# Weight copies moved to ScalarE, more idle products in the front, and three result tiles added by TensorE in a one-core language-model tower

## The reference

```python
h = emb(x) + b + positions
h = h + gelu(2 * Re(xs @ C~) + D * u)        # u = layernorm(h), xs = scan of Lambda_bar over time
x = layernorm(h)
logits = x @ router_w.T + router_b           # top 2 of 8 experts, softmax of the two
h1, h2 = split(x @ fc1_w[e].T + fc1_b[e])    # 256 each
y = (silu(h1) * h2) @ fc2_w[e].T + fc2_b[e]
h = h + sum over the token's 2 experts of weight * y
```

## Time and profile before

| | us |
|---|---|
| median of 3 runs | 154.09 |
| the three runs | 153.95, 154.09, 155.47 |
| the profiled execution's own time | 154.8 |
| its span (first to last instruction) | 153.1 |
| PE / DVE / ACT / POOL busy | 121.7 / 114.4 / 73.3 / 91.7 |
| mean granted TensorE clock (1 is full) | 0.899 |

### The profile page before, as it was taken

One profiled execution on the slowest core, in us unless ns is written; L12 is line 12 of the kernel. 1 busy time (PEld: TensorE's weight loads), 2 busy tenths in 40 slices (PEclk: granted clock), 3 DMA queues, 4 the chain that ended last, 5 costly groups with the idle time before them and its releaser, 6 DMA issues.

```text
span 153.1 us, 3532 instructions
## 1 busy us (share of the span) xinstructions
PE 121.7 (80%) x807; PEld 96.7 (63%) x807; DVE 114.4 (75%) x481; ACT 73.3 (48%) x236; POOL 91.7 (60%) x113
## 2 busy tenths in 40 slices
PE   0088889988699949966877999999999999999200
PEld 0033357476479617843765799999999999972000
DVE  2988899998994899697476768677777787735573
ACT  2063462463273142256263466878778778760000
POOL 5777779101774477157757777777777777674000
PEclk9999999986975895699999999999999999997555
DMA  4422121991441261135224414433433011100997
GB/s 106 131 52 50 38 51 34 220 297 40 148 150 52 52 227 47 44 88 116 60 75 118 91 52 113 119 106 107 121 79 82 24 42 47 54 33 0 288 310 224
DMA packets 15093, 15.65 MB, mean 102 GB/s; under 512 B 2995, under 2 KB 11701, under 8 KB 15074
## 3 DMA queue, kind: packets, MB, share of 16 engines
q1 hardware_dynamic: 10914, 9.39, 23.4%
q0 software_dynamic: 2784, 5.28, 10.8%
q10 hardware_dynamic: 1376, 0.77, 1.7%
HBM read 9.62 MB, written 6.27 MB: 104 GB/s over the span
## 4 chain that ended last, share of the span: by engine, by line
PE 23%; issue 9%; DVE 6%; POOL 6%; DMA 5%; DVEq 1%; SPq 1%; ACT 1%; POOLq 0%; ACTq 0%
PE bank L1220 7%; PE bank L1206 7%; PE bank L1196 6%; POOL results L363 6%; DMA yres<-results 3%; DVE act_h L752 1%; PE bank L1186 1%; DMA results<-ysb,dest 1%; SPq L279 1%; DVEq L738 1%; DVE res L844 1%; DVE res L848 1%; PE bank L1076 1%; ACT rows L904 1%; DVE arg L634 0%
## 5 line engine op out<-in xcount | busy, mean ns | idle before, releaser
L352 POOL DMA_INDIRECT sorted_rows<-rows,slot x32 | 32.3, 1010 | 27.2 <-DVE slot L654 18.2
L741 DVE COPY w1b<-w_sb 128x516 f32 x39 | 18.5, 476 | 13.2 <-issue 5.3
L752 DVE SCALAR_TENSOR_TENSOR act_h<-bank,w1b,sil 128x128 f32<-128x128 f32 x78 | 23.6, 343 | 5.0 <-PE bank L1206 1.4
L363 POOL DMA_INDIRECT results<-ysb,dest x22 | 21.7, 986 | 7.9 <-issue 7.3
L1220 PE MATMUL bank<-w_sb,act_h 128*128 x156 | 24.7, 281 | 1.5 <-issue 1.0
L1206 PE MATMUL bank<-xT,w1b 128*128 128x128 f32 x156 | 24.1, 277 | 1.5 <-DVE act_h L752 1.4
L953 ACT ACTIVATE sil<-bank,w1b 128x128 f32<-128x128 f32 x78 | 24.4, 364 | 0.1
L1196 PE MATMUL bank<-xT,w1b 128*128 128x128 f32 x156 | 24.0, 276 | 0.0
L1220 PEld LDWEIGHTS bank<-w_sb,act_h 128*128 128x128 f32 x156 | 20.5, 191 | 2.7 <-issue 2.6
L1206 PEld LDWEIGHTS bank<-xT,w1b 128*128 128x128 f32 x156 | 20.5, 192 | 2.1 <-DVE act_h L752 2.1
L944 ACT COPY xT<-bank 128x128 f32<-128x128 f32 x39 | 10.3, 265 | 22.4 <-PE bank L1186 22.3
(11 more groups left out here) (231 smaller groups left out, 185.5 us busy)
## 6 DMA issues: line engine op xcount, KB each, us to landing
w_sb<-w_all SPq DMA_DIRECT2D x8, 386.0 KB, 4.9
xt<-sorted_rows SPq DMA_DIRECT2D x39, 65.0 KB, 1.9
yres<-results SPq DMA_DIRECT2D x8, 256.0 KB, 4.7
sorted_rows<-pad SPq DMA_DIRECT2D x1, 520.0 KB, 5.9
sorted_rows<-rows,slot POOLq DMA_INDIRECT x32, 2.8
out<-res SPq DMA_DIRECT2D x2, 256.0 KB, 3.9
results<-ysb,dest POOLq DMA_INDIRECT x22
results<-ysb,xt POOLq DMA_INDIRECT x17
```

The costliest lines, as they stand in the source:

```text
L352: gp.indirect_dma_start(sorted_rows[:, :], bass.IndirectOffsetOnAxis(ap=slot[:, k, t:t + 1], axis=0), rows[:, k, t, :], None).then_inc(s_s ...
L363: gp.indirect_dma_start(results[:, :], bass.IndirectOffsetOnAxis(ap=target, axis=0), ysb[i][:, :], None, bounds_check=bound, oob_is_err=Fa ...
L741: v.tensor_copy(w1b[i % 4][:, :], w_sb[:, bass.ds(at, W1)]).then_inc(s_wb, 1)
L752: v.scalar_tensor_tensor(act_h[i % 2][:, q], ps_l[sides(i)][:, q], w1b[i % 4][:, 2 * HID + 2 + c:2 * HID + 3 + c], sil[i % 2][:, q], ALU.a ...
```

## The change

Three things at once.

1. The nine weight copies of the first list (tiles 0 to 8) are made by ScalarE, not VectorE. ScalarE waits for the table of tile numbers and for the weights, loads nine register values in one go, copies tile 0's weights before `gelu(3)`, those of 1 and 2 after it, of 3 after `turn_copy(2)` and before `normed_x(3)`, and of tile i+3 in the loop for i = 1 to 5, before `keep(i - 1)`. VectorE starts with tile 9.
2. `idle_products` are put in: 3 after `turn_u(2)`, 6 after `skipped(2)`, 3 after `logits(1)`, 11 where 3 stood before `turn_x(2)` (a wait that stood there is gone), 5 after `list_tiles(0)`, 4 where 1 stood before `rotated(3, 0)`.
3. Tiles 36 to 38 are no longer scattered and loaded back (`SPREAD` is 3, `STORED` 36). GpSimd makes counting rows, VectorE makes a 0/1 matrix for each of the 3 tiles and 4 groups (`spread_tile`, 128x512 each), and TensorE adds `spread.T @ ysb` into the PSUM bank of the group's bias term, 4 products of 128x128x128 fp32 for each tile and group. As rows that only these tiles hold are no longer written, SP first fills `results` (2 MB) with zeros from a tile that VectorE clears; GpSimd waits for that before its first result. The bias terms use four banks; VectorE's additions now go group by group.

```diff
+SPREAD = 3
+STORED = NTILES - SPREAD
-        ps_add = [banks[0], banks[6]]
+        ps_add = [banks[0], banks[6], banks[2], banks[5]]
...
+            sp.wait_ge(s_zero, 1)
+            sp.wait_ge(s_gath[1], 16 * GT)
+            sp.dma_start(results[:, :].rearrange("(p q j) d -> p q (j d)", p=P, j=GT),
+                         zeros[:, None, :].to_broadcast([P, K * NT // GT, GT * D])).then_inc(s_empty, 16)
             sp.wait_ge(s_const, 3)
...
-            sp.wait_ge(s_ys, 16 * NTILES)
+            sp.wait_ge(s_ys, 16 * STORED)
...
+            gp.iota(iota_j[:, :, :], [[1, GT], [GT, P]], base=0, channel_multiplier=0,
+                    allow_small_or_imprecise_dtypes=True).then_inc(s_iotaj, 1)
...
+            pool.wait_ge(s_empty, 16)
             scatter_result(0)
             scatter_result(1)
             scatter_rows(NG - 1)
-            for i in range(2, NTILES):
+            for i in range(2, STORED):
                 scatter_result(i)
...
+            def last_tokens():
+                dve.wait_ge(s_dest, chunk_of(NTILES - 1) - chunk_of(EARLY) + 1)
+                dve.wait_ge(s_iotaj, 2)
+                step(v.tensor_copy(last_d[:, :], dest[:, LATE - SPREAD:LATE]))
+                step(v.tensor_scalar(last_h[:, :], last_d[:, :], TOKENS - 0.5, -float(TOKENS), ALU.is_gt, ALU.mult))
+                step(v.tensor_tensor(last_d[:, :], last_d[:, :], last_h[:, :], ALU.add))
+                v.tensor_tensor(last_g[:, :, :], last_d[:, :, None].to_broadcast([P, SPREAD, NG]),
+                                iota_g[:, None, :].to_broadcast([P, SPREAD, NG]), ALU.subtract).then_inc(s_last, 1)
+
+            def spread_tile(n, g):
+                dve.wait_ge(s_last, 1)
+                v.tensor_scalar(spread[:, n, g, :], iota_j[:, :, :].rearrange("p j t -> p (j t)"),
+                                last_g[:, n, g:g + 1], None, ALU.is_equal).then_inc(s_spread, 1)
...
-            dve.wait_ge(s_table, 2)
-            dve.wait_ge(s_w, 16 * NE)
-            expert_weights(0)
-            expert_weights(1)
...
-                if i + 2 < NTILES:
+                if FULL[0] <= i + 2 < NTILES:
...
+                if i == CHUNKS[-2]:
+                    last_tokens()
+                if i == NTILES - 2:
+                    for t in range(SPREAD):
+                        spread_tile(t, 0)
+
+            for g in range(1, NG):
+                for t in range(SPREAD):
+                    spread_tile(t, g)
             for g in range(NG):
                 add_bias(g)
-            for g in range(NG):
                 dve.wait_ge(s_added, g + 1)
...
+            def first_list():
+                act.wait_ge(s_table, 2)
+                act.wait_ge(s_w, 16 * NE)
+                return nc.values_load_multi_w_load_instructions(
+                    tile_wi[0:1, 0:FULL[0]], engines=[mybir.EngineType.Activation], min_val=0, max_val=(NE - 1) * WE,
+                    skip_runtime_bounds_check_because="starts of an expert's weights, made from the expert's number")[1]
+
+            def copy_weights(i):
+                if i >= 4:
+                    act.wait_ge(s_a, 2 * i - 6)
+                a.copy(w1b[i % 4][:, :], w_sb[:, bass.ds(starts[i], W1)]).then_inc(s_wa, 1)
...
+            starts = first_list()
+            copy_weights(0)
             gelu(3)
+            copy_weights(1)
+            copy_weights(2)
...
                 if i == 0:
+                    copy_weights(3)
                     normed_x(3)
                     copy_xnT(3)
+                if 1 <= i and i + 3 < FULL[0]:
+                    copy_weights(i + 3)
...
             turn_u(2)
+            idle_products(3, ps_xT[1])
             b_times_u(2)
             skipped(2)
+            idle_products(6, ps_xT[1])
             turn_x(1)
             logits(1)
+            idle_products(3, ps_xT[1])
             rotated(2, 0)
...
-            pe.wait_ge(s_xnT, 4)
-            idle_products(3, ps_xT[1])
+            idle_products(11, ps_xT[1])
             turn_x(2)
             logits(2)
             list_tiles(0)
+            idle_products(5, ps_xT[1])
             pe.wait_ge(s_rotin, NG)
-            idle_products(1, ps_vs)
+            idle_products(4, ps_vs)
...
+            def spread_result(n, g):
+                pe.wait_ge(s_oe, STORED + n + 1)
+                pe.wait_ge(s_spread, SPREAD * g + n + 1)
+                for j in range(GT):
+                    ins = te.matmul(ps_add[g][:, j * D:(j + 1) * D], spread[:, n, g, j * P:(j + 1) * P],
+                                    ysb[STORED + n][:, :], start=False, stop=(n == SPREAD - 1 and j == GT - 1))
+                if n == SPREAD - 1:
+                    ins.then_inc(s_corr, 1)
...
+                if i == NTILES - 2:
+                    mixed_bias(0)
             for g in range(NG):
-                mixed_bias(g)
+                if g >= 1:
+                    mixed_bias(g)
+                for t in range(SPREAD):
+                    spread_result(t, g)
```

More of the change, by code:

```diff
@@ L190, in lm_tower @@
         ysb = [sb(f"ysb{i}", [P, D]) for i in range(NTILES)]
+        zeros = sb("zeros", [P, GT * D])
+        iota_j = sb("iota_j", [P, GT, P])
+        iota_g = sb("iota_g", [P, NG])
+        last_d = sb("last_d", [P, SPREAD])
+        last_h = sb("last_h", [P, SPREAD])
+        last_g = sb("last_g", [P, SPREAD, NG])
+        spread = sb("spread", [P, SPREAD, NG, GW])
         yres = sb("yres", [P, K, NT, D])
@@ L217, in lm_tower @@
         s_corr = sem("s_corr"); s_added = sem("s_added")
+        s_zero = sem("s_zero"); s_empty = sem("s_empty"); s_iotaj = sem("s_iotaj"); s_last = sem("s_last"); s_spread = sem("s_spread")
         s_norm = sem("s_norm"); s_un = sem("s_un"); s_uTp = sem("s_uTp"); s_uT = sem("s_uT")
@@ L226, in lm_tower @@
         s_xt = [sem(f"s_xt{i}") for i in range(NTILES)]
-        s_tp = sem("s_tp"); s_te = sem("s_te"); s_wb = sem("s_wb"); s_gate = sem("s_gate"); s_lin = sem("s_lin")
+        s_tp = sem("s_tp"); s_te = sem("s_te"); s_wa = sem("s_wa"); s_wb = sem("s_wb"); s_gate = sem("s_gate"); s_lin = sem("s_lin")
         s_sil = sem("s_sil"); s_a = sem("s_a"); s_op = sem("s_op"); s_oe = sem("s_oe")
@@ L234, in lm_tower, with copied @@
         out_rows = out.rearrange("b s d -> (b s) d")
+        def copied(i):
+            return (s_wa, i + 1) if i < FULL[0] else (s_wb, i - FULL[0] + 1)
         def group_rows(dram, first):
@@ L341, in _ @@
             gp.tensor_tensor(e, e, pos_sb[:, :, :], ALU.add).then_inc(s_emb, 1)
+            gp.iota(iota_j[:, :, :], [[1, GT], [GT, P]], base=0, channel_multiplier=0,
+                    allow_small_or_imprecise_dtypes=True).then_inc(s_iotaj, 1)
+            gp.iota(iota_g[:, :], [[GW, NG]], base=0, channel_multiplier=0,
+                    allow_small_or_imprecise_dtypes=True).then_inc(s_iotaj, 1)
             bound = pool.alloc_register("last_result")
@@ L419, in taylor_sum @@
                                                   ALU.mult, ALU.add))
+            v.memset(zeros[:, :], 0.0).then_inc(s_zero, 1)
             dve.wait_ge(s_prm, 16)
@@ L738, in expert_weights @@
                 at = dve.value_load(tile_wi[0:1, i:i + 1], min_val=0, max_val=(NE - 1) * WE)
-                if i >= 4:
-                    dve.wait_ge(s_a, 2 * i - 6)
+                dve.wait_ge(s_a, 2 * i - 6)
                 v.tensor_copy(w1b[i % 4][:, :], w_sb[:, bass.ds(at, W1)]).then_inc(s_wb, 1)
@@ L745, in gated @@
                     if c == 0:
-                        dve.wait_ge(s_wb, i + 1)
+                        dve.wait_ge(*copied(i))
                         dve.wait_ge(s_lin, i + 1)
@@ L778, in add_bias @@
                 e = res[:, GT * g:GT * g + GT, :].rearrange("p j d -> p (j d)")
-                v.tensor_tensor(e, e, ps_add[g % 2][:, :], ALU.add).then_inc(s_added, 1)
+                v.tensor_tensor(e, e, ps_add[g][:, :], ALU.add).then_inc(s_added, 1)
             positions_bias()
@@ L947, in gate @@
                 act.wait_ge(s_gate, i + 1)
-                act.wait_ge(s_wb, i + 1)
+                act.wait_ge(*copied(i))
                 if i >= 2:
@@ L1188, in first @@
             def first(i):
-                pe.wait_ge(s_wb, i + 1)
+                pe.wait_ge(*copied(i))
                 pe.wait_ge(s_te, i + 1)
@@ L1237, in mixed_bias @@
                     pe.wait_ge(s_te, NTILES)
-                if g >= 2:
-                    pe.wait_ge(s_added, g - 1)
-                te.matmul(ps_add[g % 2][:, :], mixT[:, g, :], bias_d[:, :, :].rearrange("p j d -> p (j d)"),
-                          start=True, stop=True).then_inc(s_corr, 1)
+                if g == 2:
+                    pe.wait_ge(s_sil, 2 * NTILES)
+                te.matmul(ps_add[g][:, :], mixT[:, g, :], bias_d[:, :, :].rearrange("p j d -> p (j d)"),
+                          start=True, stop=False)
+            def spread_result(n, g):
[6 more added lines that the diff above has]
+                    ins.then_inc(s_corr, 1)
             pe.wait_ge(s_table, 2)
```

## The result

Five runs of each kernel, in turn on one chip: before 155.38 us (median), after 156.63 (156.04 to 158.72). The ratio of after to before is 1.0175, 95% interval 1.011 to 1.0241: slower, by 1.2 us by the medians and 2.7 by the ratio. Forecast were 153.1, a range of 151.0 to 155.5, and 15% for slower by over 1%. The profiled execution of after is its slowest (158.72; span 157.0, 1.7 outside it): its clock stood at 0.50 between 71 and 81 us, which some later profiles don't show, so of it the front and the end are read, and not the first tiles.

A forecast was written before the change was run, and what follows sets the result against it. No engine bounded everything: TensorE tiles 10 to 37, VectorE the front mostly, scatter, reload and additions the end. Terms -1.9 - 2.3 + 3.0 = -1.2; 1.0 subtracted from the 154.09 median gave 153.1 us, range 151.0 to 155.5.

The forecast's parts named there:

- Term: +3.0, bounds +2.3 and +3.7: At the end: TensorE's fp32 products for the last three tiles replace the reload as limit, 3.0 us slower.
- Term: -1.9: In the front: idle products hold the clock, cutting VectorE's wait before `find_slots(1)`; 1.9 us faster, bounds -2.3 and +1.0.
- I take it that the clock holds: In the front: six idle products ahead of the clock's fall keep it full, costing nothing where TensorE sat idle.
- Term: -2.3: Early tiles: moving VectorE's register loads and weight copies to ScalarE saves 2.3 us, bounds -3.1 and -1.0.
- The 3.1 us that I counted at tiles 4 to 6: VectorE's register loads and copies between router step and `gated`: 3.1 us together, all saved if ScalarE is ready.
- the ring: Not forecast: `second` waits for `keep`, behind a copy, behind `turn_copy`, which needs `turn`, queued behind the previous `second`.
- the rival of 4.5 us: Before `gelu(3)`: ScalarE's nine-register list takes 4.5 us and delays the first tiles; +0.8, 154.9 us, chance 0.13.
- The clock is not held: In the front: idle products gain nothing and stand in the way; +1.3, 155.4 us, chance 0.12.
- Both gains whole, tail cheap: Whole kernel: idle products -1.9, copies -3.1, tail only +2.3; -2.7, 151.4 us, chance 0.20.
- The zeros delay the gathers of group 2: In the front: the zero fill slows these gathers and with them `scan(1)`; +1, 154.1 us, chance 0.08.

The follow-up runs named there:

- f4: Only the 2 MB zero fill of `results` and VectorE's clearing of its source, on the kernel before: 155.37 us against 154.89, ratio 0.9938.
- f1: Only the last three tiles added by TensorE, with the zeros, on the kernel before: 159.36 us against 154.89, ratio 1.0304.
- g2: f3 plus all idle products of the change: 152.48 us against 154.93 for the kernel before, ratio 0.9881.
- h1: The whole change as made, measured again against the kernel before: 157.25 us against 155.07.
- h4: h3 plus all idle products of the change: 152.08 us against 155.07 for the kernel before.
- h3: h2 with the spread products in bf16, each result split into two halves: 153.82 us against 155.07 for the kernel before.
- g4: The whole change, but with the weight copy of tile i+3 behind `keep(i-1)`: 155.63 us against 154.93 for the kernel before, ratio 1.0163.
- h2: g4 without the new idle products: 155.96 us against 155.07 for the kernel before.
- f3: Only ScalarE's weight copies, with that of tile i+3 behind `keep(i-1)`, on the kernel before: 152.26 us against 154.89, ratio 0.9854.
- g1: Only ScalarE's weight copies, in the change's order (ahead of `keep(i-1)`), on the kernel before: 153.13 us against 154.93, ratio 1.0003.
- f2: As f1 but with one last tile in place of three (`SPREAD` 1): 155.95 us against 154.89 for the kernel before, ratio 1.009.

## Why the prediction was wrong

**The tail, "Term: +3.0, bounds +2.3 and +3.7".** This step failed; the mechanism was right, the size short. From tile 37's second product, which starts at the same time in both traces (135.57, 135.60), it is +4.0. By its parts in the trace of after: the first spread products at 137.71 (forecast 137.84); 96 instructions in 2.84 + 3 x 2.94, which without the overlap are 11.5 and not 10.6, for I had taken the tile stage's 0.111 and they need 0.12; three bias products at 1.05 and not 0.85, 0.6 more (in before two stood back to back, here each stands between spread products); hand-over 0.05, not 0.3. Why 0.12 and not 0.111 is open. Alone, with the zeros (taken at 0; +0.5 by f4's median, nothing by its trace), f1 measured +4.5, 1.5 over the term and 0.8 over its upper bound.

**The idle products, "Term: -1.9".** This step failed too. "I take it that the clock holds" came true in the profile, but the wait was not the whole path: it fell by 2.2 while VectorE came 1.15 later. Of these, 0.4 was there at `scan(1)` (29.13 for 28.73; the rows of group 2 were taken after a wait of 0.22 for their gather, beside the zeros), 0.4 more came with a longer wait for TensorE at `find_slots(0)` (0.74 for 0.34), and the last 0.36 in `scan(2)`, where VectorE waited 0.46 for its own step. g2, without zeros and spread tiles, had neither the first nor the last and gained the whole 2.1. After gained 1.0. Then came two things that weren't in the sum. The clock's loss and return vary from execution to execution: the gain at `find_slots(1)` was 1.2 to 2.1 where it had dipped before 40 us (g2 against before; after and h1 against f1; h4 against h3) and 0.1 where it hadn't (g4 against h2). And in all four profiles with all the idle products and full clock in the front (after, g2, h1, h4) the clock was low from 70 to 80 us, which goes with tile 4 up to 3.2 later. By medians the term is 0 (g4 against h2, g2 against f3). The prediction called the clock full till 40.70, and the earlier trace rows show the dip ahead of that. What makes it dip stays open; so does the prediction's point that transposes don't count for it, which no run isolates.

**The copies, "Term: -2.3".** By size nearly right (g1 -1.8 by median), by its working only in part, and so partly by luck. The 3.1 us that I counted at tiles 4 to 6 left out copies 0 to 2, worth 1.5 at tile 0; I hadn't seen the ring (0.75), nor that GpSimd, at 1.29 a scatter, would bound the end as soon as TensorE was 3 us early (f3's tail is 1.1 longer). The register list took one load of 0.97 us (at 60.2), and `gelu(3)` began at 62.85: the rival of 4.5 us is wrong.

**The sum** of what was measured, -1.8 + 4.5 + 0 = +2.7, agrees with the ratio of after (+2.7) and with h1 (+2.2), and is above the median's +1.2; each term is known to half a us or so, so the agreement is no closer than that. That three terms were each larger than their sum was stated; an error of 1.5 in one and 1.9 in another turned it.

**The rivals.** "The clock is not held", which was to end at +1.3, came nearest in outcome, and by chance: its 1.3 was made of other terms than the measured ones, and the clock was held in the front and lost behind it. "Both gains whole, tail cheap" had the tail at its lower bound, furthest from what came. "The zeros delay the gathers of group 2" took place in part: in after the eight gathers landed after 4.3 us (2.6 in before), and `scan(1)` came 0.4 later, not 1.

## What to carry to other kernels

Moving work from a transfer to an engine pays only if the engine's own instructions for it, counted one by one at the price of the same type and shape, take less time than the transfer did; here 96 fp32 instructions did not, and 96 in bf16 did, by 0.9 us of the tail. Before a gain in one engine is passed on to the end, look which queue runs without idle time right below it (GpSimd's 1.29 under TensorE's 1.45), and which additions were hidden in a wait that the change removes (f2). Compare two profiles from the last step that the edit can't have touched: here 0.9 of the 2.4 us at tile 0 in f3 lay ahead of it. In an in-order queue, place new work behind the step that frees what another engine waits for.

## What the runs showed of the hardware

- A 128x128x128 product in fp32 is two instructions. Each took 0.12 us in the spread products (0.24 in all) and 0.111 on the mean of the tile stage; in bf16 it is one of 0.056.
- The six filling products kept the clock when 0.32 us of idle time followed and not when 1.04 did, but the clock had also dipped before in the first case and not in the second (0.83 and 1.00 from 30 to 40 us). A full clock in the front came together with a clock of 0.50 to 0.66 twenty microseconds later in after, g2, h1 and h4. What decides either stays open; no run varied only this.
- Up to `find_slots(1)` nearly the same instructions ran in two ways from one execution to another: with the clock at 0.83 from 30 to 40 us (before, f1, h3) the step came at 50.19 to 50.80, with 1.00 there (f2, f3, f4, g1, h2) at 49.27 to 49.69.
- A list of nine registers on ScalarE is one load of 0.97 us, against nine of 0.30 on VectorE.
- Two megabytes of zeros beside the gathers of group 2 took 7.8 us in f4, and the eight gathers in that time landed after 3.6 us (median), for 2.6 of the same eight in before; in after it was 4.3.
- Indirect scatters of 128 rows, issued without a wait, follow each other on GpSimd every 1.29 us: 0.98 busy and 0.30 between (f3).
